# Last layer of a four-layer graph network: neighbour sums as two float32r products instead of one float32 product

## The reference

```python
msgs = x[src]
summed = jax.ops.segment_sum(msgs, dst, num_segments=x.shape[0])
deg = jax.ops.segment_sum(jnp.ones_like(dst, dtype=x.dtype), dst, num_segments=x.shape[0])
neighbor_mean = summed / jnp.maximum(deg, 1.0)[:, None]
message = jnp.concatenate([x, neighbor_mean], axis=-1)
weighted = jnp.einsum('of,nf->no', w, message)
return jax.nn.relu(weighted)
```

## Time and profile before

| what | value |
|---|---|
| median of 3 runs | 1691.36 us (1691.3 to 1697.8) |
| span of the profiled execution | 1690.4 us |
| median of the runs less that span | 1.0 us |
| TensorE busy, of the span | 1478.5 us (87%) |
| VectorE, ScalarE, GpSimd busy | 1306.6, 739.0, 498.2 us |
| count products L1306 | 200 records, 592 ns mean |

### The profile page before, as it was taken

How to read it: one execution, slowest core, us unless ns; L and a number is a source line. 1 busy time by engine, 2 the same in 40 slices (tenths; PEclk the granted TensorE clock), 3 DMA queues, 4 the chain that set the end, 5 groups by cost and what they waited for, 6 DMA issues and landing times.

```text
span 1690.4 us, 24268 instructions
## 1 busy us (share of the span) xinstructions
PE 1478.5 (87%) x7869; PEld 805.5 (48%) x7869; DVE 1306.6 (77%) x2051; ACT 739.0 (44%) x1580; POOL 498.2 (29%) x496
## 2 busy tenths in 40 slices
PE   2888998367888787899999999979999999999997
PEld 1465445213333335566555565855544444444443
DVE  8786999997999997499898999697577656632232
ACT  1285666267555555355454555441244333402000
POOL 1788888710011012356555664000000000002000
PEclk9988999678999997799999999979999999999999
DMA  4101000143121102466565667000111201220000
GB/s 143 42 6 9 6 7 7 36 146 114 43 68 40 65 16 82 129 184 183 165 183 165 182 184 148 1 1 26 50 50 50 70 30 58 66 74 1 13 19 30
DMA packets 66890, 122.06 MB, mean 72 GB/s; under 512 B 12753, under 2 KB 31299, under 8 KB 66702
## 3 DMA queue, kind: packets, MB, share of 16 engines
q0 software_dynamic: 23408, 59.71, 14.1%
q1 hardware_dynamic: 41976, 57.57, 10.5%
q10 hardware_dynamic: 1446, 4.03, 0.7%
HBM read 105.85 MB, written 15.23 MB: 72 GB/s over the span
## 4 chain that ended last, share of the span: by engine, by line
PE 53%; DVE 16%; POOL 14%; issue 10%; ACT 4%; DMA 2%; DVEq 1%; ACTq 0%; POOLq 0%
PE PS L1240 18%; POOL recs L656 14%; PE PS L1116 8%; DVE arena L1923 6%; PE PS L1205 5%; PE PS L1306 5%; PE PS L1102 5%; DVE arena L1919 3%; ACT arena L1578 3%; PE PS L1291 2%; PE PS L1302 2%; PE PS L1167 1%; DVE cnt_d L1704 1%; DVE arena L2123 1%; PE PS L976 1%
## 5 line engine op out<-in xcount | busy, mean ns | idle before, releaser
L1240 PE MATMUL PS<-arena 128*125 128x512 f32 x640 | 275.0, 592 | 0.0
L656 POOL DMA_INDIRECT recs<-arena x170 | 244.3, 1437 | 89.9 <-issue 89.0
L1578 ACT ACTIVATE arena<-arena,gslot 128x32 f32<-128x32 f32 x832 | 185.1, 308 | 172.5 <-PE PS L1116 89.6
L1116 PE MATMUL PS<-arena 128*32 128x128 f32 (+1 forms) x3328 | 235.0, 311 | 16.2 <-issue 8.0
L721 POOL DMA_INDIRECT arena<-xup,gidx x208 | 197.5, 949 | 147.6 <-issue 69.9
L1116 PEld LDWEIGHTS PS<-arena 128*32 128x32 f32 x3328 | 176.9, 111 | 127.1 <-issue 68.6
L1028 PE MATMUL PS<-arena 125*128 125x512 f32 (+1 forms) x480 | 190.5, 534 | 44.1 <-DVE arena L1923 43.9
L2072 DVE TENSOR_TENSOR arena<-PS,arena 128x768 f32<-128x768 f32 x208 | 196.7, 946 | 0.0
L1240 PEld LDWEIGHTS PS<-arena 128*125 128x125 f32 x640 | 120.1, 188 | 154.6 <-issue 154.1
L1028 PEld LDWEIGHTS PS<-arena 125*128 125x128 f32 x480 | 86.0, 191 | 148.4 <-issue 78.0
L728 POOL CAST arena<-cnt_s 125x1250 f32<-125x1250 uint16 x10 | 12.5, 1302 | 473.1 <-PE PS L1240 473.1
(11 more groups left out here) (341 smaller groups left out, 2149.9 us busy)
## 6 DMA issues: line engine op xcount, KB each, us to landing
arena<-in_spline_wT SPq DMA_DIRECT2D x16, 1024.0 KB, 5.4
arena<-uv_rows SPq DMA_DIRECT2D x14, 610.4 KB
arena<-h_rows SPq DMA_DIRECT2D x26, 256.0 KB
h_rows<-arena SPq DMA_DIRECT2D x24, 256.0 KB, 2.8
arena<-xup,gidx POOLq DMA_INDIRECT x208
recs<-arena POOLq DMA_INDIRECT x170
xup<-arena SPq DMA_DIRECT2D x10, 250.0 KB
out<-x_sb SPq DMA_DIRECT2D x10, 250.0 KB
```

Of the source, the lines that this page charges most:

```text
L656: pool.indirect_dma_start(out=recs, out_offset=bass.IndirectOffsetOnAxis(pos[:, c:c + 1], 0), in_=rec[:, c, :], in_offset=None).then_inc(s ...
L1116: ins = t.matmul(PS[quad * DB:(quad + 1) * DB, bank, o0 * MUL:o0 * MUL + w], sel4[:, s, v * DB:(v + 1) * DB], prod[:, s, c0 * MUL:c1 * MUL ...
L1240: return t.matmul(PS[:NP, y2_bank(half, b), :], lhs[:, (k * HB + b) * NP:(k * HB + b + 1) * NP], w[:, k * D:(k + 1) * D], start=(first and ...
L1578: ins = A(sel4[:, s, y * DB:(y + 1) * DB], eq4[:, m // 4, s * DB:(s + 1) * DB], ACT.Copy, scale=gslot[:, par, c + R_Y + y:c + R_Y + y + 1])
```

## The change

The neighbour product takes its operands as float32r (four bytes in memory, multiplied with a shortened mantissa). z is written twice: ScalarE writes `z_hi`, rounded to float32r, VectorE writes `z_lo`, z less `z_hi`, also float32r (`z_low`). Each of the 100 count products becomes two, one with `z_hi` and one with `z_lo`, both with the same float32r `cnt50` block. Counts are exact in that type up to 4096. For source nodes with more than 4096 outgoing edges (at most 8 could exist, found at run time) the row is zeroed in `cnt50` by a factor `keep`, and an eleventh product per block adds it back: up to 8 such rows in four copies of 32 partitions, the count split in two 8- and 7-bit parts by masks, the z row in its two pieces, gathered from DRAM copies `cnt_rows` and `z_rows` by indirect DMA. That product is always issued.

Order: the eight spline steps of the second half are written out instead of a loop; VectorE counts out-degrees (five reductions of 2500 counts) during steps 1 to 5; two tiny matmuls stand before the last step and two behind the first transposes. z uses six PSUM banks. The self products of three blocks come before the first neighbour product, and then run three blocks ahead.

The ten casts became ten multiplications at the same place, and two gathers follow them in GpSimd's queue. The diff, cut to what the prediction speaks of (the semaphores of the transposes were also merged, with no change of order):

```diff
@@ sp
             spline_weights(1, 0)
+            sp.dma_start(cnt_rows.rearrange("(b p) n -> p b n", p=NP), cnt_s[:]).then_inc(s_cntrow_out, 16)
...
+            for b in range(NB):
+                sp.wait_ge(s_z_cp, b + 1)
+                sp.dma_start(z_rows[b * NP:(b + 1) * NP, :], z_hi[:NP, b, :].bitcast(f32)).then_inc(s_zrow_out, 16)
+                sp.wait_ge(s_zlo_ok, b + 1)
+                sp.dma_start(z_rows[N + b * NP:N + (b + 1) * NP, :], z_lo[:NP, b, :].bitcast(f32)).then_inc(s_zrow_out, 16)
@@ gpsimd
             pool.wait_ge(s_sp_free, 2 + 2 * NSPL)
+            pool.wait_ge(s_big_ok, 1)
             for k in range(NB):
-                pool.tensor_copy(cnt50[:, k, :], cnt_s[:, k, :]).then_inc(s_p3_ok, 1)
+                pool.tensor_scalar(cnt50[:NP, k, :], cnt_s[:, k, :], keep[:, k:k + 1], None, ALU.mult).then_inc(s_p3_ok, 1)
...
@@ tensor
-            with pe.Fori(0, NSPL // 2) as i:
+            for i in range(NSPL // 2):
                 for par in range(2):
                     spline_step(1, i, par)
+                    if 2 * i + par == NSPL - 2:
+                        pe.wait_ge(s_big_ok, 1)
+                        t.matmul(PS[:NP, 0, 0:NB], upper[:NP, :NP], big[:], start=True, stop=True)
+                        t.matmul(PS[:NP, 0, 16:16 + NB], ones[:NP, 0:NP], big[:], start=True, stop=True).then_inc(s_big_ps, 1)
...
-                if c == 1:
-                    pe.wait_ge(s_y2_cp, HB + 1)
-                if c >= 2:
-                    pe.wait_ge(s_z_cp, c - 1)
+                if c < HB:
+                    pe.wait_ge(s_y2_cp, HB + c + 1)
+                if c == HB:
+                    pe.wait_ge(s_big_ok, 3)
+                if c >= len(ZB):
+                    pe.wait_ge(s_zlo_ok, c - len(ZB) + 1)
...
-            pe.wait_ge(s_z_cp, NB)
-            pe.wait_ge(s_wl2_in, 80)
-            for b in range(NB):
+            def near_part(b):
                 if b >= 2:
                     pe.wait_ge(s_y3_cp, b - 1)
-                for k in range(KT):
-                    t.matmul(PS[:NP, 4 + b % 2, :], xT3[:, k, b * NP:(b + 1) * NP], w_self[:, k, :], start=(k == 0), stop=(k == KT - 1))
                 for k in range(NB):
                     if b == 0:
                         pe.wait_ge(s_p3_ok, k + 1)
-                    ins = t.matmul(PS[:NP, b % 2, :], cnt50[:, k, b * NP:(b + 1) * NP], z_sb[:, k, :],
-                                   start=(k == 0), stop=(k == NB - 1))
-                ins.then_inc(s_y3_ps, 1)
+                    for z, first in ((z_hi, k == 0), (z_lo, False)):
+                        t.matmul(PS[:NP, 3 * (b % 2), :], cnt50[:NP, k, b * NP:(b + 1) * NP], z[:NP, k, :], start=first, stop=False)
+                if b == 0:
+                    pe.wait_ge(s_big_ok, 4)
+                    pe.wait_ge(s_z_cp, NB + 1)
+                t.matmul(PS[:NP, 3 * (b % 2), :], big_cnt[:, b * NP:(b + 1) * NP], big_z[:], start=False, stop=True).then_inc(s_y3_ps, 1)
+            pe.wait_ge(s_wl2_in, 80)
+            pe.wait_ge(s_zlo_ok, HB + 1)
+            for b in range(len(SB4) - 1):
+                self_part(b)
+            pe.wait_ge(s_zlo_ok, NB)
+            for b in range(NB):
+                near_part(b)
+                if b + len(SB4) - 1 < NB:
+                    self_part(b + len(SB4) - 1)
@@ scalar
-                A(z_sb[:, b, :], PS[:NP, 3 * (b % 2), :], ACT.Copy).then_inc(s_z_cp, 1)
+                A(z_hi[:NP, b, :], PS[:NP, ZB[b % len(ZB)], :], ACT.Copy).then_inc(s_z_cp, 1)
...
+            act.wait_ge(s_bigrow_in, 32)
+            A(big_z[:], big_zrow, ACT.Copy).then_inc(s_z_cp, 1)
@@ vector
+                    n = 2 * i + par
+                    if 1 <= n <= HB:
+                        ks = slice(2 * (n - 1), 2 * n)
+                        ins = v.tensor_reduce(outdeg[:, ks], cnt_s[:, ks, :], X, ALU.add)
...
+            def rows_big():
+                dve.wait_ge(s_bigrow_in, 16)
+                dve.wait_ge(s_big_ok, 3)
+                v.tensor_scalar(big_row[0:64], big_row[0:64], 0x7F80, None, ALU.bitwise_and)
+                link(v.tensor_scalar(big_row[64:128], big_row[64:128], 0x7F, None, ALU.bitwise_and))
+                v.tensor_scalar(big_cnt[:], big_row, bvalid[:], None, ALU.mult).then_inc(s_big_ok, 1)
+            def z_low(b):
+                dve.wait_ge(s_z_cp, b + 1)
+                v.tensor_tensor(z_lo[:NP, b, :], PS[:NP, ZB[b % len(ZB)], :], z_hi[:NP, b, :], ALU.subtract).then_inc(s_zlo_ok, 1)
...
+            index_big()
...
+            for b in range(NB):
+                z_low(b)
+                if b == HB:
+                    rows_big()
```

More of the change, by code:

```diff
@@ L47 @@
 AHEAD = 3
+EXACT = 4096
+MAXBIG = 8
+ZB = (3, 4, 5, 6, 7, 0)
+SB4 = (1, 2, 7, 6)
+assert E // (EXACT + 1) <= MAXBIG
 assert NB % WR == 0 and G % 4 == 0
@@ L110, in build @@
         xup = dram("xup", (N, D))
+        cnt_rows = dram("cnt_rows", (N, N), u16)
+        z_rows = dram("z_rows", (2 * N, D))
         x_sb = sb("x_sb", [NP, NB, D])
+        cnt_at = -(-nc.sbuf_base // 32) * 32
         cnt_all = sb("cnt_d", [128, NB * SPAN], u16)
@@ L135, in build @@
         epsc = sb("epsc", [128, 1])
+        outdeg, big, keep = (sb(name, [NP, NB]) for name in ("outdeg", "big", "keep"))
+        btot, bend, bslot = (sb(name, [NP, NB]) for name in ("btot", "bend", "bslot"))
+        bsel, bnode = sb("bsel", [NP, NB, MAXBIG]), sb("bnode", [NP, NB, MAXBIG])
+        blist, bred = sb("blist", [NP, 2, 128]), sb("bred", [NP, 2, MAXBIG])
+        node_no = sb("node_no", [NP, NB])
+        bidx_c, bidx_z, bvalid = sb("bidx_c", [128, 1], u32), sb("bidx_z", [128, 1], u32), sb("bvalid", [128, 1])
         mv = sb("mv", [NP, NB, 2])
@@ L281, in build @@
         cslot = sb("cslot", [128, 2])
[L283 to L287, removed]
+        w_self = at(0, [128, KT, D])
+        w_near = at(16848, [128, KT, D])
+        cnt50 = nc.alloc_sbuf_tensor_at("cnt50", [128, NB, N], f32r, offset=arena_at + 4 * 4328)
+        z_hi = nc.alloc_sbuf_tensor_at("z_hi", [128, NB, D], f32r, offset=arena_at + 4 * 18896)
+        z_lo = nc.alloc_sbuf_tensor_at("z_lo", [128, NB, D], f32r, offset=cnt_at)
+        big_z = nc.alloc_sbuf_tensor_at("big_z", [128, D], f32r, offset=cnt_at + 4 * NB * D)
+        big_cnt = nc.alloc_sbuf_tensor_at("big_cnt", [128, N], f32r, offset=arena_at + 4 * 3072)
+        big_row = cnt_all[:, 2 * (NB + 1) * D:2 * (NB + 1) * D + N]
+        big_zrow = at(29020, [128, D])
+        fin = at(2048, [NP, 2, D])
+        xT3 = at(24016, [128, KT, N])
         s_acc_done = sem("s_acc_done")
@@ L437, in build @@
         s_z_cp = sem("s_z_cp")
+        s_zlo_ok = sem("s_zlo_ok")
+        s_big_ok = sem("s_big_ok")
+        s_big_ps = sem("s_big_ps")
+        s_cntrow_out = sem("s_cntrow_out")
+        s_zrow_out = sem("s_zrow_out")
+        s_bigrow_in = sem("s_bigrow_in")
         s_z_ps = sem("s_z_ps")
@@ L640, in _ @@
             pool.iota(cen[:], pattern=[[1, NSPL]], base=0, channel_multiplier=0, allow_small_or_imprecise_dtypes=True)
+            pool.iota(node_no[:], pattern=[[NP, NB]], base=0, channel_multiplier=1, allow_small_or_imprecise_dtypes=True)
             pool.wait_ge(s_const0, 1)
@@ L726, in _ @@
             pool.wait_ge(s_sp_free, 2 + 2 * NSPL)
+            pool.wait_ge(s_big_ok, 1)
             for k in range(NB):
-                pool.tensor_copy(cnt50[:, k, :], cnt_s[:, k, :]).then_inc(s_p3_ok, 1)
+                pool.tensor_scalar(cnt50[:NP, k, :], cnt_s[:, k, :], keep[:, k:k + 1], None, ALU.mult).then_inc(s_p3_ok, 1)
+            pool.wait_ge(s_big_ok, 3)
+            pool.wait_ge(s_cntrow_out, 16)
+            pool.nop(nofuse=True)
+            pool.indirect_dma_start(out=big_row, out_offset=None, in_=cnt_rows,
+                                    in_offset=bass.IndirectOffsetOnAxis(bidx_c[:, 0:1], 0)).then_inc(s_bigrow_in, 16)
+            pool.wait_ge(s_zrow_out, 16 * 2 * NB)
+            pool.nop(nofuse=True)
+            pool.indirect_dma_start(out=big_zrow, out_offset=None, in_=z_rows,
+                                    in_offset=bass.IndirectOffsetOnAxis(bidx_z[:, 0:1], 0)).then_inc(s_bigrow_in, 16)
         @block.tensor
@@ L733, in _ @@
             t = nc.tensor
-            def transposes(src, ready, done, copied, banks, copied0=0):
-                for b in range(NB):
[L738 to L741, removed]
-                    for k in range(KT):
[L743 to L755, removed]
             def uv_transposes(src, nr, done, b0):
@@ L1295, in _, with self_part @@
                     x3_transposes(c + 2)
-            pe.wait_ge(s_z_cp, NB)
-            pe.wait_ge(s_wl2_in, 80)
-            for b in range(NB):
+            def self_part(b):
+                if b >= len(SB4):
+                    pe.wait_ge(s_y3_cp, b - len(SB4) + 1)
+                for k in range(KT):
+                    t.matmul(PS[:NP, SB4[b % len(SB4)], :], xT3[:, k, b * NP:(b + 1) * NP], w_self[:, k, :],
+                             start=(k == 0), stop=(k == KT - 1))
```

(18 more changed lines are left out.)

80 lines of the change are left out of this document (49 added, 31 removed).

## The result

| | before | changed |
|---|---|---|
| median, us | 1692.59 (4 runs, 1691.3 to 1697.8) | 1673.65 (4 runs, 1668.14 to 1675.73) |
| ratio to before | | 0.9887, interval 0.9855 to 0.9918 |
| span of the profiled execution, us | 1690.4 | 1672.1 |
| from the first transpose behind the last spline step to the end, us | 170.8 | 151.0 |

Faster by 18.9 us, where 41 were forecast; 1673.65 lies just above the range's 1672.

What follows compares the result with a forecast made beforehand. TensorE bounds the last stage: -85.9 (float32 count products) - 0.9 (wait) + 45.2 (float32r products) + 0.5 (tiny matmuls) = -41.1 us, taking the span from 1690.4 to 1649.3 and the median to 1650, range 1643 to 1672.

Steps and rivals of the forecast that it cites:

- The path of the gathered rows: Last z_lo, its DMA, gather and ScalarE copy end at 1570.6, before the product needing them at 1574.0: 3 us cover.
- stands still d once: Last stage: if the gathered rows come late by d, TensorE waits that long a single time.
- The distance: Float32r neighbour products in the last stage start 0.215 us apart, 210 of them adding 45.2 us.
- my bounds: GpSimd's ten multiplications cost between one and three times the 1.30 us cast; up to 5 us each stays hidden.
- the removed wait before the self products: TensorE's wait between z and the self products, with the cold start behind it, goes: 0.9 us saved.
- the reductions beside the spline steps: VectorE's five out-degree reductions, 2.6 us each, lie beside TensorE's spline steps and cost nothing.
- the tiny products: Four tiny float32 matmuls: two before the last spline step add 0.4 us, two behind the first transposes 0.1 at most.
- the write of `cnt_rows`: DMA of 3.1 MB behind a 1 MB load, about 12 us, done before the next weights are needed: costs nothing.
- the last three blocks: At the end blocks come every 4.5 us, VectorE needs about 3.9 and keeps up; the tail stays 10.3 us.
- Rival 1: Neighbour products: four-byte columns stream at half rate, 0.429 us per product, 1695 us, no change; chance 0.09.
- Rival 3: Neighbour products: float32r runs at the float32 price, two records of 0.43 us, slower at 1785 us; chance 0.05.
- Rival 2: Last stage: TensorE waits for gathered rows, counts or weight loads, giving back 5 to 24 us, 1655 to 1674; chance 0.06.

Runs made afterwards that it cites:

- e6_rows_late: Changed kernel with VectorE's three instructions on big_row moved behind the last z_low: 1670.84 us, ratio 0.9868 to the kernel before.
- e7_dve_counts: Changed kernel with each z write split into 112 and 13 rows, and VectorE instead of GpSimd making the counts: 1651.90 us, ratio 0.9786 to before.
- e2_cast: Changed kernel with GpSimd casting the counts instead of multiplying them by keep: 1665.07 us, ratio 0.9823 to the kernel before.

## Why the prediction was wrong

Within the stage I forecast 170.8 - 41.5 = 129.3 us (the 0.4 us of two tiny products lies ahead of it); it took 151.0. The terms of the 21.7:

- **The path of the gathered rows: 13.8 us, the step that failed.** I wrote "z_lo of block 9 at about 1561, its DMA to DRAM 5.2 us" and found 3 us of cover. That is the price of one transfer into an empty queue. There are twenty, each 250 KB and 2.0 us; all but the first wait for `z_low`, which starts at 1543, so from 1544 the queue holds the path, to 1585.7. The 5.2 us came from output blocks that leave some 12 us apart and never queue. I priced the latency and never the rate. (The z_lo of block 9 was late too, at 1569.4 in place of 1561, behind VectorE's wait for the count rows; by `e6_rows_late` that cost nothing.)
- **The low clock behind the stop: 3.1 us.** 1590.49 to 1597.25 against 0.23 + 3.44. I had written that TensorE "stands still d once", and left out what the stop costs after it.
- **The distance: 210 x (0.232 - 0.215) = 3.6 us.** The mechanism was right (one pass, one record), the size off by 8%.
- **GpSimd: 1.3 us directly.** 3.53 us per multiplication lay inside my bounds of one to three times 1.30, and under the 5 us I called hidden. What it did elsewhere I had not priced: VectorE's scaling of x beside it took 1.98 us, once 3.50, in place of the 0.65 to 0.92 beside the casts:

```profile
1530.38 0.92 DVE L2196 TENSOR_SCALAR x_sb<-x_sb,mv,rstd 125x512 f32<-125x512 f32 x1
...
1536.10 3.50 DVE L2241 TENSOR_SCALAR x_sb<-x_sb,mv,rstd 125x512 f32<-125x512 f32 x1
1540.44 2.50 DVE L2316 TENSOR_SCALAR deg<-deg 125x10 f32<-125x10 f32 x1
```

(the first is of before; the last took 0.17 there). So the z products got a wait of 1.0 us and a slower start behind it, and from the first transpose to the last z it took 40.6 us, against 39.3 in `e7_dve_counts` and before, and z_low started at 1543 instead of some 1536, which is the 5.4 us of the wait by `e2_cast`, already in the first term.

They add up to 21.8, the 21.7 but for rounding.

Right were: the cost of a count product before (0.859), the removed wait before the self products, the reductions beside the spline steps (2.75 us each, no wait of TensorE), the tiny products (0.34 us for the first two, 0.4 said), the write of `cnt_rows` at no cost seen, and the last three blocks, whose chain is TensorE alone. Rival 1, four bytes at half rate with 1695 us, is out: 0.45 ns per column, not 0.85. The Trainium skill's 614 GB/s for the moving operand ("SBUF — State Buffer", A bandwidth-pool intuition that's wrong) is stated there for bfloat16, and to read it as a bound for four-byte data, as the prediction did for rival 1, was wrong here: 4 bytes x 125 lanes in 0.453 ns are 1104 GB/s. The Trainium skill's four passes for true FP32 ("FP8 and Floating Point Precision", TensorE Precision Notes) agree with 0.859 / 0.216 = 4.0 against bfloat16; against float32r it is 0.859 / 0.232 = 3.7. Rival 3 is out too. Rival 2, to which I gave 0.06, is what happened, by its first named way: the stop, the slow products behind it and the wait in z gave back 18.2 us, inside its 5 to 24. With the 3.6 us of the distance, which it had not in it, the time still lay inside its 1655 to 1674, but above 1672, where my range ended.

## What to carry to other kernels

A side path that ends in one late product is priced by every queue that it goes through, rate times count from its first start, not by the latency of its last piece. Look at the rate of a DMA and the share of engines that it keeps busy: the same bytes as 112 and 13 rows went at twice the rate of 125 rows. An edit on an engine "with time to spare" has to be checked for what stands behind it in its queue and for what another engine does more slowly beside it. And a chain of waits through an issuing engine doesn't say that the DMA queue behind it was empty.

## What the runs showed of the hardware

- DMAs of 125 rows of 2 KB, queued, moved at 126 to 128 GB/s with a third of the DMA engines busy and five small packets each; as 112 and 13 rows they moved at 242 to 273 GB/s with seven to eight tenths busy, and the last output block landed in 1.9 us in place of 5.2 to 5.7. That five engines carry the 125 rows is inferred from these. Other row counts weren't tried, nor any other cut in two, so whether it is the 112 or the cut itself that spreads the rows isn't shown.
- float32r products of 512 columns stand 0.232 us apart, of 256 columns 0.118, bfloat16 ones of 512 columns 0.216. The records of the weight loads, 185 ns each, overlap one another at 0.118, so their length isn't what a load costs the next product.
- Behind stops of TensorE of 13.8, 8.4 and 0.5 us the next four self products took 6.00, 5.07 and 3.43 us; in the first stop the granted clock fell from 1.00 to 0.50.
- VectorE's SBUF to SBUF tensor_scalar of 125x512 took 0.55 us alone, 0.65 to 1.26 beside GpSimd's casts and 1.98 to 3.50 beside its 3.53 us multiplications (one of 125x10 took 2.50 in place of 0.17), as if it waited for the end of one; instructions that read PSUM, and the statistics, did not change.
